# Local attention: query and key columns in natural order, and scores by one matmul per head and block of 32 queries

## What is computed

```python
q = l2norm(q) * qs                     # per head, over 64 channels
k = l2norm(k) * ksc
q = q * cos * scale + rotate_half(q) * sin * scale
k = k * cos / scale + rotate_half(k) * sin / scale
bk2, bv2 = look(bk), look(bv)          # window w and the one before: 64 keys
sim = einsum('bhwie,bhwje->bhwij', bq, bk2) * 8.0
sim = where(mask, -max, sim)
attn = softmax(sim, -1)
out = einsum('bhwij,bhwje->bhwie', attn, bv2)
x = out @ Wo + x                       # q, k, v come from shift_tokens(x) @ Wqkv
```

## Time and profile before

| what | us |
|---|---|
| median of 3 runs | 4794.62 (4789.98 to 4795.23) |
| the profiled execution | 4798.22 |
| its span, first to last instruction | 4796.1 |
| mean granted clock of TensorE | 0.903 |

### The profile page before, as it was taken

The page is one execution under the profiler, slowest core; times in us unless marked ns, Lnnn a source line. Parts: engine busy times, 40 slices in busy tenths (PEclk is TensorE's granted clock), DMA queues, the critical chain, the costliest instruction groups (busy, mean ns, idle before and its releaser), DMA issues. The chain is left out here.

```text
span 4796.1 us, 87181 instructions
## 1 busy us (share of the span) xinstructions
PE 3964.9 (83%) x31240; PEld 3141.4 (65%) x31432; DVE 3055.9 (64%) x4550; ACT 2319.4 (48%) x4509; POOL 1813.8 (38%) x1572
## 2 busy tenths in 40 slices
PE   4666589889889889889889858999988976567998
PEld 1224378678678678778778638888888864225555
DVE  6894578378379378378478366655565535885554
ACT  4442268578468568568568523333232222542222
POOL 2560067167157157257257213333333211562000
PEclk7998789999999999999999969998888778897999
DMA  0000011011011011011011000000000000001000
GB/s 13 0 0 15 6 50 31 23 38 31 21 36 32 22 36 31 23 34 32 23 35 32 9 5 4 1 4 4 4 4 4 2 5 6 0 0 53 0 0 9
DMA packets 56422, 81.14 MB, mean 17 GB/s; under 512 B 13146, under 2 KB 32628, under 8 KB 54900
## 3 DMA queue, kind: packets, MB, share of 16 engines
q1 hardware_dynamic: 56052, 75.99, 5.3%
HBM read 30.87 MB, written 1.05 MB: 7 GB/s over the span
## 5 line engine op out<-in xcount | busy, mean ns | idle before, releaser
L1624 POOL TENSOR_TENSOR local_rot<-local_term 128x512 f32<-128x512 f32 x384 | 482.7, 1278 | 643.2 <-DVE local_term L1944 643.2
L1944 DVE TENSOR_TENSOR local_term<-bank,local_table 128x512 f32<-128x512 f32 x768 | 485.2, 674 | 125.4 <-ACT local_sq L1828 125.4
L1113 POOL TENSOR_TENSOR delta_lt_n<-delta_lt,delta_joint 128x512 f32<-128x512 f32 x224 | 289.7, 1324 | 423.2 <-PE bank L1198 263.1
L1630 POOL TENSOR_TENSOR local_rot<-local_rot,local_inv 128x512 f32<-128x512 f32 x384 | 392.8, 1044 | 147.9 <-ACT local_inv L1839 147.5
L272 POOL TENSOR_TENSOR mamba_hc<-mamba_state,mamba_c_all 128x512 f32<-128x512 f32 x256 | 319.6, 1270 | 309.6 <-DVE mamba_state L451 304.1
L1665 PE MATMUL bank<-local_w_layer,local_xs 128*128 128x256 f32 x1536 | 401.2, 406 | 26.2 <-issue 20.0
L1867 ACT ACTIVATE local_attn<-bank 64x256 f32<-64x256 f32 x768 | 290.6, 378 | 205.9 <-PE bank L1719 199.1
L1665 PEld LDWEIGHTS bank<-local_w_layer,local_xs 128*128 128x128 f32 x1536 | 287.9, 198 | 75.6 <-issue 29.2
L1399 DVE TENSOR_TENSOR delta_x_all<-delta_x_all,bank 128x512 f32<-128x512 f32 x160 | 109.9, 687 | 349.3 <-PE bank L1208 349.3
L1719 PE MATMUL bank<-local_pt,local_v_moved 64*128 64x64 f32 x3072 | 313.5, 281 | 0.0
L1719 PE MATMUL bank<-local_pt,local_v_at 64*128 64x64 f32 x3072 | 304.3, 275 | 0.0
(11 more groups left out here) (350 smaller groups left out, 9347.7 us busy)
## 6 DMA issues: line engine op xcount, KB each, us to landing
local_v_moved<-local_v_at SPq DMA_DIRECT2D x192, 192.0 KB, 2.4
local_w_layer<-a_w_layer_dram SPq DMA_DIRECT2D x6, 1536.0 KB, 6.4
local_v_moved<-local_v_at SPq DMA_DIRECT2D x192, 32.0 KB, 2.1
moe_w<-f_w_dram SPq DMA_DIRECT2D x3, 2048.0 KB, 15.6
local_w_o<-a_w_o_dram SPq DMA_DIRECT2D x12, 256.0 KB, 3.9
local_w_up<-a_w_up_dram SPq DMA_DIRECT2D x6, 341.0 KB, 4.1
moe_w<-f_w_dram SPq DMA_DIRECT2D x3, 576.0 KB, 4.8
delta_w_h<-g_w_qkv_dram SPq DMA_DIRECT2D x8, 192.0 KB, 2.3
```

What stands on the lines that cost most here:

```text
L1113: pool.tensor_tensor(lt_n[:, lv % 2, n, :, :], lt[:, n, :, :], joint[:, lv, :].unsqueeze(1).to_broadcast([P, QUAD, C]), ALU.mult).then_inc ...
L1624: pool.tensor_tensor(rot[:, i % 2, :, :, f, :], here[:, :, f, :, :], there[:, :, 1 - f, :, :], ALU.add).then_inc(summed, 1)
L1630: pool.tensor_tensor(one, one, spread(inv[:, i % 2, tiles, :].rearrange("p t x -> p (t x)"), E), ALU.mult).then_inc(normalized, 1)
L1944: dve.tensor_tensor(term[:, which, b, :], g.bank[b][:, :], table[:, which, :, :].rearrange("p n c -> p (n c)"), ALU.mult).then_inc(roped, 1)
```

## The change

The query and key columns keep their natural order (head, half, channel), in the weights, scales and tables laid out on the host and so in banks 0 and 1, squares and terms. The squares of a head's 64 channels are then neighbours: each of two reductions sums over 64, and half_sums, the wait for both and the addition are gone. q_rot is half as wide and is copied in one piece, without zeros. The scores take one matmul per head and block of 32 queries: 64 channels x 32 queries as weights, the same 64 keys as moving data, 32 matmuls instead of 16, each writing 32 partitions of bank 3. The wait for the keys comes through wait_apart. The diff, its contexts cut:

```diff
@@ -1458,7 +1458,7 @@
         one = [np.stack([8 * w * scale] * 2 + [w / scale] * 2, 1) for w in halves]
-        terms.append(np.stack(one, 1).reshape(T // P, P, 2 * P))
+        terms.append(np.stack(one, 2).reshape(T // P, P, 2 * P))
     return np.stack(terms, 2).transpose(1, 2, 0, 3).astype(np.float32)
@@ -1492,7 +1492,7 @@
         xs = sb("xs", [P, BATCH, W + T])
-        q_rot = sb("q_rot", [P, 2, 2 * GROUP])
+        q_rot = sb("q_rot", [P, 2, GROUP])
         k_rot = sb("k_rot", [P, 2, SPG, W + T])
@@ -1501,9 +1501,8 @@
         term = sb("term", [P, 2, SPG, GROUP])
-        rot = sb("rot", [P, 2, TPG, 4, 2, W])
-        half_sums, sums_q = sb("half_sums", [P, SPG, 2, 2, 4]), sb("sums_q", [P, TPG, 4])
-        logs_q, inv = sb("logs_q", [P, TPG, 4]), sb("inv", [P, 2, TPG, 4])
+        rot = sb("rot", [P, 2, TPG * 4, 2, W])
+        sums_q, logs_q, inv = sb("sums_q", [P, TPG * 4]), sb("logs_q", [P, TPG * 4]), sb("inv", [P, 2, TPG * 4])
         most, total = sb("most", [P, 2, 2 * TPG]), sb("total", [P, 2, 2, 2 * TPG])
@@ -1528,7 +1527,7 @@
         dve_own, act_own, act_ln, pool_own = sem("dve"), sem("act"), sem("act_ln"), sem("pool")
-        act_passed, sp_passed = sem("act_passed"), sem("sp_passed")
+        act_passed, sp_passed, pe_passed = sem("act_passed"), sem("sp_passed"), sem("pe_passed")
         block = ctx.enter_context(nc.Block())
@@ -1558,7 +1557,7 @@
 
-            return buf.rearrange("p b (n f x c) -> p (b n) f x c", n=2, f=2, c=W)
+            return buf.rearrange("p b (x f c) -> p (b x) f c", f=2, c=W)
 
@@ -1596,7 +1595,6 @@
             own.step(pool.memset(k_rot[:, :, :, 0:W], 0.0))
-            own.step(pool.memset(q_rot[:, :, :], 0.0))
             own.step(pool.memset(v_moved[0:W, :, :], 0.0))
@@ -1621,13 +1619,13 @@
                 for f in range(2):
-                    pool.tensor_tensor(rot[:, i % 2, :, :, f, :], here[:, :, f, :, :], there[:, :, 1 - f, :, :], ALU.add).then_inc(summed, 1)
+                    pool.tensor_tensor(rot[:, i % 2, :, f, :], here[:, :, f, :], there[:, :, 1 - f, :], ALU.add).then_inc(summed, 1)
                 pool.wait_ge(inv_ready, s + 1)
...
                 for b in range(SPG):
-                    tiles = slice(2 * b, 2 * b + 2)
-                    one = rot[:, i % 2, tiles, :, :, :].rearrange("p t x f c -> p (t x) (f c)")
-                    pool.tensor_tensor(one, one, spread(inv[:, i % 2, tiles, :].rearrange("p t x -> p (t x)"), E),
+                    heads = slice(8 * b, 8 * b + 8)
+                    one = rot[:, i % 2, heads, :, :].rearrange("p x f c -> p x (f c)")
+                    pool.tensor_tensor(one, one, spread(inv[:, i % 2, heads], E),
                                        ALU.mult).then_inc(normalized, 1)
@@ -1679,7 +1677,7 @@
                     for k in range(TPG):
-                        src = rot[:, i % 2, k, H * which:H * (which + 1), :, :]
+                        src = rot[:, i % 2, 4 * k + H * which:4 * k + H * (which + 1), :, :]
                         mm = pe.transpose(bank[:, k * P:(k + 1) * P], src.rearrange("p h f c -> p (h f c)"), g.ident[:, :])
@@ -1688,15 +1686,17 @@
                 pe.wait_ge(q_copied, s + 2)
-                pe.wait_ge(k_copied, s + 2)
+                wait_apart(pe, k_copied, s + 2, pe_passed)
                 for b in range(SPG):
-                    for w in range(WINDOWS):
-                        n, half, r = w // 4, w // 2 % 2, w % 2
-                        column = ((b * 2 + n) * 2 + half) * 2 * W
-                        query = (b * WINDOWS + w) * H * W
-                        mm = pe.matmul(S_BANK[H * W * r:H * W * (r + 1), column:column + 2 * W],
-                                       q_rot[:, i % 2, query:query + H * W], k_rot[:, i % 2, b, w * W:(w + 2) * W],
-                                       start=False, stop=True, skip_group_check=True)
+                    for x in range(WINDOWS // 2):
+                        column = (b * (WINDOWS // 2) + x) * 2 * W
+                        for r in range(2):
+                            for hh in range(H):
+                                ch, w = slice(E * hh, E * (hh + 1)), 2 * x + r
+                                query = b * T + w * W
+                                row = H * W * r + W * hh
+                                mm = pe.matmul(S_BANK[row:row + W, column:column + 2 * W], q_rot[ch, i % 2, query:query + W],
+                                               k_rot[ch, i % 2, b, w * W:(w + 2) * W], start=False, stop=True, skip_group_check=True)
                 mm.then_inc(s_ready, 1)
@@ -1834,17 +1834,13 @@
                 act.wait_ge(sums_ready, s + 2)
-                act.activation(logs_q[:, :, :], sums_q[:, :, :], ACT.Ln, bias=guard[:, 0:1], scale=LN_SCALE).then_inc(act_ln, 1)
+                act.activation(logs_q[:, :], sums_q[:, :], ACT.Ln, bias=guard[:, 0:1], scale=LN_SCALE).then_inc(act_ln, 1)
                 act.wait_ge(act_ln, s + 2)
-                act.activation(inv[:, i % 2, :, :], logs_q[:, :, :], ACT.Exp, bias=unscale[:, 0:1], scale=-0.5).then_inc(inv_ready, 1)
+                act.activation(inv[:, i % 2, :], logs_q[:, :], ACT.Exp, bias=unscale[:, 0:1], scale=-0.5).then_inc(inv_ready, 1)
 
...
                 act.wait_ge(q_turned, s + 1)
-                for hh in range(H):
-                    ch = slice(E * hh, E * (hh + 1))
-                    ins = act.activation(q_rot[ch, i % 2, :].rearrange("p (x h q) -> p x h q", h=H, q=W)[:, :, hh, :],
-                                         Q_BANK[ch, :].rearrange("p (x q) -> p x q", q=W), ACT.Copy)
-                ins.then_inc(q_copied, 1)
+                act.activation(q_rot[:, i % 2, :], Q_BANK[:, :], ACT.Copy).then_inc(q_copied, 1)
                 act.wait_ge(k_turned, s + 1)
@@ -1933,7 +1929,7 @@
                 dve.sem_inc(free, n)
-            STEPS = 4
+            STEPS = 2
 
@@ -1944,14 +1940,11 @@
 
-            def add_squares(own, s):
+            def add_squares(s):
+                dve.wait_ge(act_ln, s + 1)
                 for b in range(SPG):
-                    own.add(dve.tensor_reduce(half_sums[:, b, :, :, :].rearrange("p n f x -> p (n f x)"),
-                                              sq[:, b, :].rearrange("p (x c) -> p x c", c=W), AX.X, ALU.add))
-                own.settle()
-                sums = half_sums[:, :, :, :, :].rearrange("p b n f x -> p (b n) f x")
-                dve.wait_ge(act_ln, s + 1)
-                dve.tensor_tensor(sums_q[:, :, :], sums[:, :, 0, :], sums[:, :, 1, :], ALU.add).then_inc(sums_ready, 1)
+                    ins = dve.tensor_reduce(sums_q[:, 8 * b:8 * b + 8], sq[:, b, :].rearrange("p (x c) -> p x c", c=E), AX.X, ALU.add)
+                ins.then_inc(sums_ready, 1)
 
@@ -1998,7 +1991,7 @@
                         rope(first + i, b, 1)
-                    add_squares(own, first + i)
+                    add_squares(first + i)
                 for i in range(SLOTS):
@@ -2017,7 +2010,7 @@
                         rope(s + 2, 1, 1)
-                        add_squares(own, s + 2)
+                        add_squares(s + 2)
                 assert own.count == SLOTS * STEPS, own.count
@@ -2110,13 +2103,13 @@
 
-    def by_halves(w):
-
-        return w.reshape(6, D, 8, 2, 2, 32)
+    def by_pair(w):
+
+        return w.reshape(6, D, 8, P)
     w_q, w_k, w_v = (i["L1_ffn_Wqkv"][:, :, 1024 * n:1024 * (n + 1)] for n in range(3))
-    w_qk = np.stack([by_halves(w_q), by_halves(w_k)], 3).transpose(0, 1, 2, 5, 3, 4, 6).reshape(6, D, 8, 2 * P)
-    w_layer = np.concatenate([w_qk, w_v.reshape(6, D, 8, P)], 3)
-    scales = np.stack([i[f"L1_ffn_{n}_scale"].reshape(6, 2, 32) for n in "qqkk"], 2).reshape(6, 1, 2 * P)
+    w_qk = np.concatenate([by_pair(w_q), by_pair(w_k)], 3)
+    w_layer = np.concatenate([w_qk, by_pair(w_v)], 3)
+    scales = np.stack([i[f"L1_ffn_{n}_scale"] for n in "qqkk"], 1).reshape(6, 1, 2 * P)
     b1 = np.zeros((6, 2, 3 * P), np.float32)
```

## The result

The changed kernel takes 4724.25 us (median of 4 runs, 4706.24 to 4727.04), the kernel before 4794.92 (4 runs): ratio 0.9845, 95% interval 0.9819 to 0.9872, 1.5% faster. Predicted were 4731 us and 1.3%, with a range of 4720 to 4800. The profiled execution took 4727.04 us, 71.2 less than the 4798.22 of before.

A forecast was written before the change was run, and what follows sets the result against it. PE's queue was taken to bound a slot, held up through ACT and POOL by DVE's addition. 40 + 3.6 + 18 + 3.6 + 1.9 - 3 = 64 us off 4798.2 gave 4734, as median 4731 us; range 4720 to 4800.

The forecast's parts named there:

- Steady slots: Local attention slots after a layer's start: without DVE's addition PE's wait for POOL goes, 40 us over six layers.
- 7.56 us is PE's time for its own work: Score to score in a slot: 7.56 us is PE's own work, the rest is DVE's small addition.
- What is late next is nothing: Steady slots without the addition: no other engine holds PE up, since POOL's L1630 ended just as PE came.
- The third rival: The wait moves: POOL or another engine is late by as much; edges and half of 40 us kept, about 4755; chance 0.08.
- PE's scores: Score matmuls of a slot: 64 records on four tiles take the same 1.15 us as 32 did, plus a small later start.
- the ramp: Score matmuls: tiles three and four start later, at most 0.02 us a slot, a loss of 3 us in all.
- Two at a time: Rival on the scores: PE overlaps only two records whatever the number of tiles; 184 us on top, 4915 us; chance 0.17.
- Fed too slowly: Rival on the scores: at 11 ns per instruction they take 0.4 us longer, no change, about 4795 us; chance 0.07.
- Layer starts: Start of a layer, where PE waits for the first two slots' chain: scores 3.0 us sooner, 18 us over six layers.
- the wait for the keys in slot 1: Slot 1 of each layer: PE waits for the key copy and gains the merged copy's 0.6 us, 3.6 us in all.
- Set-up: Before the stage starts: the zeroing of q_rot leaves POOL's chain, 1.9 us with its wait.
- Slot 30: Slot 30 of each layer: PE comes early and gains what ACT gains, some 0.6 us, 3.6 us in all.

The follow-up runs named there:

- one_input_sum: The kernel before with only the last addition on DVE written as a reduction of one operand; 4732.59 us against 4811.04, ratio 0.9842.
- norms_between: The changed kernel with ACT's Ln and Exp of the norms moved between copy_out's second and third copies; 4707.46 us, ratio 0.9808 to the kernel before.
- heads_apart: The changed kernel with all of head 0's score matmuls before head 1's, so two column tiles of one row half alternate; 4855.44 us.
- windows_apart: The changed kernel with score matmuls ordered by even and odd windows, so the two row halves alternate on one PSUM bank; 4838.36 us.
- tiles_apart: The changed kernel with score matmuls ordered so that 16 records in a row go to one tile; 5089.87 us.
- order_only: The changed kernel with the scores, q_rot, its two copies and zeroing of before, keeping natural column order and one sum; 4733.07 us, ratio 0.9839.

## Why the prediction was right, and where it was not

*Steady slots.* The addition that sat out POOL's L1624 was what paced the slots: predicted 40 us, measured 36.7, and one_input_sum gets 38.0 with nothing else changed. What is missing from the 40 is slot 1 of each layer, counted as steady: the six take 7.97 to 8.28 us, 3.6 us more in all than at 7.56, and PE still waits for POOL there (0.64 us before L1681 in the third layer). The other 168 lie between 7.553 and 7.560. "In the earlier trace rows it fell between the two" is too simple: in both rows the addition starts 1.23 us after L1624. Of the 186 additions that start within 12 ns of one of POOL's, 126 are long and 60 short; which of the two goes first is not decided by anything that the trace shows. With two operands in SBUF the addition lasts until POOL's addition ends in 132 of 192 slots (1.28 to 1.32 us in 126 of them), with one it takes 0.19 us in all of them; by what means one engine holds up the other no run shows.

*"So 7.56 us is PE's time for its own work."* This sentence failed, by 0.05 us for the wide scores and 0.10 for the new ones. I took loads that start 0.01 us behind the last for loads without a wait. But the shortest of the 174 steady slots of before took 7.553, so none was without a wait, and the row without one, in norms_between, has the loads overlap by 0.08 us. "What is late next is nothing" falls with it: late next is ACT's chain, since copy_out waits for PE's L1719, and the norms for copy_out. The third rival had named this tie, "L1630 already ended only as PE came". It cost nothing in the sum, because I had subtracted only down to 7.56 and added nothing for faster scores; the forecast of 7.56 to 7.60 a slot held (mean 7.575, median 7.553).

*PE's scores.* I took 1.15 us and the ramp's 0.02; it was 1.10, the first to last record 0.882 against 0.930. Each tile takes 64 columns every 56 ns, the wide ones took them every 58. The +3 us of the ramp never came, and the gain of 0.05 us vanished in the loop. Two at a time is refuted: fours start together, at 0, 7, 13 and 20 ns. Of the two reasons that this rival gives, starts in program order and turns on the bank, the starts show neither between tiles. Two at a time throughout would be 32 x 56 ns = 1.79 us, 0.86 more than the 0.930 of before and near the 0.96 that I charged. heads_apart, which runs in pairs but for the overlap in its middle, takes 1.575 us, 0.64 more, and its slots are 0.36 longer than the 7.786 of before. Fed too slowly is refuted too, at 6.5 ns between the starts of a four.

*Two row halves on one bank.* windows_apart alternates two row halves on one bank and has its pairs start 7 ns apart, as heads_apart has, and its scores take the same 1.575 us. No turns are taken.

*Layer starts and the wait for the keys in slot 1* (in the account: slot 0 to 1). 18.9 us against 18, and 3.4 against 3.6. *Set-up* 1.9 against 1.9.

*Slot 30.* Predicted -3.6, measured +2.3. "PE comes early and gains what ACT gains" looked at the wait alone. Of the kernel before, the slot 30 at clock 1.00 took 7.59 us with its addition at its short 0.18 us, and another with the same short addition took 10.78 at 0.64. The granted clock is worth 3.2 us there, the addition 0.6 (11.38 with the long one at the same 0.64), and the clock fell out differently from run to run.

*The sum.* 64 predicted, 59.6 and 68.4 measured in the local stack in two executions; slot 30, after the last scores and the layer starts differ between these two, and no edit does. The median moved by 70.7. That 4731 came within 7 us of 4724 is in part luck: slot 30 was wrong by 5.9 us, the ramp by 3, and stages that the edit doesn't touch were 12.5 us shorter in the profiled execution. What the runs bear out is the mechanism and the size of the steady slots and the layer starts.

## What to carry to other kernels

Look for a tiny operation whose time has two values in the trace, and see which engine is at work at its long one; here one operand less on DVE was worth as much as a rewrite of the weights' order, the copies and the scores. Before you call a time an engine's own, find a slot where nothing releases it or lengthen its work by a known amount and subtract: 8.147 - 0.693 and 9.533 - 2.080 agreed to 1 ns and gave what no row of the kernel itself showed.

## What the runs showed of the hardware

Four tiles of 64 rows x 32 columns work at once, each a record of 64 columns every 56 ns, the four started within 20 ns (changed kernel); the next tile's records start while the last tile's are still to come (heads_apart, tiles_apart); two row halves write one PSUM bank together, 7 ns apart (windows_apart). Read by their starts, records of different tiles leave the order of the program (a new series from 707 ns on in heads_apart and from 700 in tiles_apart, while the one before goes on to 869 and 862); within a tile no run shows that. Pairs on one row half run as fast as pairs on two (heads_apart and windows_apart have the same starts to the ns): neither rows nor bank limit anything here, only the tile. And in slot 30 the granted clock outweighed the edits: 7.55 us at 1.00 (order_only) against 10.78 at 0.64 (before, and 0.64 or 0.65 in the changed kernel).
